# Moving one half's quantisation chain forward in a two-layer decoder kernel

## The chip, the core and the metric

The kernel runs on one core of a Trainium2 chip. The core has five engines with queues of their own: TensorE (PE, matmuls and transposes into PSUM), VectorE (DVE), ScalarE (ACT), GpSimd (POOL) and SyncE (SP), which here only issues DMAs. The engines meet at semaphores. The metric is the device time of one execution in microseconds, the median of several; smaller is better.

## The reference, cut to what matters

Two decoder layers work on x of shape (4, 256, 256), each sub-layer behind a layer norm and added to x. Only the last three sub-layers matter here:

```python
x = x + causal_attention(layernorm(x))          # 16 heads of 16, output product w_out
# cross attention, 8 groups of 2 heads of 128, everything in emulated fp8:
ln_out = ln(layernorm(x)) * ln_w + ln_b
def linear(w, w_scale, in_scale):               # four "kinds": q, qx, k, v
    y = clip(ln_out / in_scale, -448, 448)      # per column
    return (fp8(bf16(y)) * in_scale) @ w.T * w_scale
q, qx, k, v = ...                               # q, qx, k are layer normed per head
core = softmax(q k^T) v;  xout = softmax(qx kx^T) vx      # kx, vx come from the context
x = x + fp8(clip(concat(core, xout) / smooth)) @ wproj.T * scale
x = x + mixture_of_experts(layernorm(x))
```

## The kernel before, in words

The 1024 tokens are two halves of two sequences each (half 0: sequences 0 and 1, half 1: sequences 2 and 3). Each engine's program is written out by hand, and each runs its queue strictly in order. PSUM has 8 banks; the table built by `plan_front` and `plan_slot` says who uses a bank in which order, and an engine that fills a bank waits until the one before has drained it.

**Causal steps.** Causal attention runs as 16 steps (`STEPS`, i = 0 to 15, eight for each half). In one step PE makes scores for step i+1 (L744 to L748), turns the probabilities of step i (L760) and averages step i-1 (L779); DVE takes the row maxima (L1575) and copies turned probabilities (L1586); ACT takes exponentials (L1153). Among these steps half 0 gets its output product `heads_out(0)` (L705, step 10), its two layer norms Q1 and Q2, the transposes of the normed tokens (L590, step 12), and its four kinds: ACT applies ln_w, ln_b (`take_affine`, L1175) and the column scales (`scale_kind`, L1186), DVE clamps and rounds (`clamp` L1605, L1608, `round_kind` L1613, L1614), and POOL makes the last subtraction into `xq` (`split`, L1995). Every 1024-wide DVE instruction there has bf16 operands in SBUF.

**Slots.** Then 32 items (group, sequence) run through a pipeline of slots o = 0 to 35. In slot n PE projects item n (`project_item`, L835, L850; two token tiles t), turns weights of a coming group (`next_weights`, L802, L804), turns the heads of item n-1 (`turn_item_heads`, L863), makes its scores (`score_item`, L889), averages item n-3 (`average_item`, L876) and makes the output product of item n-4 (L904). ACT squares projections for the head norms (L1215), copies heads (L1224, L1231), takes exponentials (L1258) and scales averages (L1246). POOL turns the sums of squares into 1/std (`head_scale`, L1982, L1983). DVE normalises heads (L1645), takes maxima (L1659), makes the low part of each weight (L1626, L1631), scales probabilities (L1670) and lays them out by a 32x32 transpose (L1676), one for each side of the item, and quantises the averaged heads (`quantise_item`, L1652 and L113 to L116).

**The move of the probabilities.** The laid tile has a single buffer. SP moves it to `probsT` by 16 DMAs an item (`move_item_probs`, L548), after both sides are laid. DVE's side 0 transpose of the next item waits until all 16 have landed:

```python
if side == 0 and before >= 0:
    v.wait_ge(probs_moved[before % 2], (before // 2 + 1) * (16 * MOVES))
```

Items 0 to 3 belong to half 0, so half 1 has time: its output product `heads_out(1)` runs at the end of slot 0, its norms in slots 0 and 1, its token transposes in slot 2, kinds 0 and 1 in slot 2, kinds 2 and 3 in slot 3. The first item of half 1 is item 4: in slot 4 `project_item` waits for each of the four splits (kinds in the order q, k, v, qx).

## Time and profile before

| | us |
|---|---|
| median of 3 runs | 998.78 (998.55 to 1000.34) |
| the profiled execution | 998.71 |
| its span in the trace | 996.9 |
| mean granted TensorE clock | 0.966 of full speed |

The span is the stretch from the first to the last traced instruction; 1.8 us of the execution's time lie around it. All positions below are in us from the span's start. The causal steps end near 295, slot 0 starts there, and the slots fill the stretch up to about 870. A row of the timeline gives start, duration, engine, line, operation, tiles and a count of merged instructions; in brackets stands the idle time of the engine before the row and who ended it. Where instructions of one row overlap or are merged, the duration is from the first start to the last end.

### The profile page before, as it was taken

Reading aid. Unit: us, or ns where it says so; the run is one execution under the profiler, and the core shown is the slowest. Engines: PE = TensorE matmul, PEld = TensorE weight load, DVE = VectorE, ACT = ScalarE, POOL = GpSimd, SP = SyncE. Lnnn points to the kernel's source line nnn. Section 1 sums busy time; section 2 is a strip of 40 time slices with the busy share of each in tenths; the row PEclk is TensorE's granted clock in tenths of the full one; section 3 lists DMA queues with packets and bytes.
Section 4 is the critical chain, followed back from the end, with each engine's and each line's share of the span. In section 5 each row is a group of like instructions: output and inputs, shape, how many; then the busy total and the mean of one; then the engine's idle time right before and its main releaser. Section 6 shows DMA issues by size and latency. Waiting matters only on the chain.

```text
span 996.9 us, 15862 instructions
## 1 busy us (share of the span) xinstructions
PE 911.4 (91%) x5254; PEld 681.3 (68%) x5254; DVE 713.1 (72%) x1549; ACT 563.8 (57%) x2101; POOL 150.5 (15%) x194
## 2 busy tenths in 40 slices
PE   5989999998879679999999999999999998789796
PEld 3647566656558567888888787878787776545453
DVE  3674545666686886887888788888888787765653
ACT  3461335446345856777877676877777776321311
POOL 2001202000033331121212111121212121000000
PEclk9999999999889879999999999999999999889898
DMA  7001000000101312232432432423422623110000
GB/s 218 1 23 42 0 1 1 2 1 1 43 1 43 85 43 55 73 94 71 113 94 55 112 81 59 129 54 75 117 70 54 198 57 78 47 43 0 22 0 21
DMA packets 64083, 56.80 MB, mean 57 GB/s; under 512 B 11201, under 2 KB 62978, under 8 KB 64002
## 3 DMA queue, kind: packets, MB, share of 16 engines
q1 hardware_dynamic: 63904, 55.76, 20.7%
q8 instruction: 42, 0.69, 0.3%
q14 instruction: 39, 0.32, 0.1%
q10 hardware_dynamic: 98, 0.03, 0.0%
HBM read 21.15 MB, written 1.05 MB: 22 GB/s over the span
## 4 chain that ended last, share of the span: by engine, by line
PE 43%; DVE 24%; SPq 18%; issue 5%; DMA 5%; ACT 4%; POOL 2%; DVEq 0%; ACTq 0%
SPq L548 18%; DVE laid L1676 6%; PE ps L956 6%; DMA group_probsT<-laid 4%; PE ps L876 4%; PE ps L835 3%; DVE group_probs L1670 3%; PE ps L889 3%; PE ps L692 2%; PE ps L682 2%; PE ps L904 2%; PE ps L705 2%; DVE neg_max L1575 2%; PE ps L850 2%; PE ps L744 2%
## 5 line engine op out<-in xcount | busy, mean ns | idle before, releaser
L1258 ACT ACTIVATE group_probs<-ps,score_bias 128x256 f32<-128x256 f32 x256 | 117.2, 484 | 55.9 <-DVE score_bias L1659 55.9
L835 PE MATMUL ps<-group_w_hi,xq 128*128 128x256 f32 (+1 forms) x512 | 133.4, 301 | 5.5 <-POOL xq L1995 5.5
L1659 DVE TENSOR_REDUCE score_bias<-ps 128x2 f32<-128x512 f32 x128 | 87.7, 691 | 59.8 <-PE ps L889 59.8
L876 PE MATMUL ps<-group_probsT,group_values 128*128 128x512 f32 x256 | 120.8, 608 | 5.1 <-DVE x_all L1683 3.0
L835 PE MATMUL ps<-group_w_lo,xq 128*128 128x256 f32 (+1 forms) x512 | 122.9, 282 | 0.0
L1215 ACT ACTIVATE group_squares<-ps 128x128 f32<-128x128 f32 x384 | 108.7, 340 | 16.4 <-PE ps L835 9.2
L889 PE MATMUL ps<-group_kT,group_qT 128*128 128x256 f32 x512 | 115.9, 379 | 0.0
L889 PEld LDWEIGHTS ps<-group_kT,group_qT 128*128 128x128 f32 x512 | 97.0, 190 | 26.6 <-issue 10.5
L835 PEld LDWEIGHTS ps<-group_w_hi,xq 128*128 128x128 f32 x512 | 100.1, 196 | 7.1 <-issue 5.6
L835 PEld LDWEIGHTS ps<-group_w_lo,xq 128*128 128x128 f32 x512 | 100.0, 195 | 1.0
L1215 ACT ACTIVATION_READ_ACCUMULATOR group_squares<-ps 128x1 f32 x384 | 97.5, 274 | 0.0
L1676 DVE STREAM_TRANSPOSE laid<-group_probs 128x1024 f32<-128x1024 f32 x64 | 79.7, 1246 | 17.4 <-DMA group_probsT<-laid 15.9
L876 PEld LDWEIGHTS ps<-group_probsT,group_values 128*128 128x128 f32 x256 | 45.5, 191 | 61.3 <-issue 45.1
L1246 ACT ACTIVATE group_cat_y<-ps,vec_inv 128x256 bf16<-128x256 f32 x128 | 53.5, 471 | 59.7 <-PE ps L876 59.7
L1983 POOL TENSOR_TENSOR head_rstd<-head_sum,minus_half 128x6 f32<-128x6 f32 x64 | 86.0, 1343 | 5.3
L904 PE MATMUL ps<-group_wp_hi,group_cat 128*128 128x256 f32 x256 | 70.0, 310 | 8.9 <-DVE group_cat L116 8.9
L1670 DVE TENSOR_SCALAR group_probs<-group_probs,score_inv 128x256 f32<-128x256 f32 x256 | 74.6, 355 | 0.5
L1982 POOL TENSOR_SCALAR head_sum<-head_sum 128x6 f32<-128x6 f32 x64 | 13.9, 218 | 401.9 <-ACT group_values L1217 401.8
L1645 DVE TENSOR_TENSOR group_heads<-ps,head_rstd 128x384 f32<-128x384 f32 x128 | 62.4, 544 | 14.9 <-POOL head_rstd L1983 14.9
L850 PE MATMUL ps<-group_w_x,ctxT 128*128 128x256 f32 x256 | 66.5, 382 | 0.0
L904 PE MATMUL ps<-group_wp_lo,group_cat 128*128 128x256 f32 x256 | 64.3, 288 | 0.0
L1224 ACT ACTIVATE group_qT<-ps,query_affine 128x512 f32<-128x512 f32 x64 | 50.5, 789 | 24.3 <-PE ps L863 24.3
(258 smaller groups left out, 1775.3 us busy)
## 6 DMA issues: line engine op xcount, KB each, us to landing
group_probsT<-laid SPq DMA_DIRECT2D x512, 64.0 KB, 2.1
group_raw_p<-in_L_xattn_wproj_dram SPq DMA_DIRECT2D x16, 256.0 KB, 3.4
group_raw_w<-in_L_xattn_wq_dram SPq DMA_DIRECT2D x8, 256.0 KB, 2.8
group_raw_w<-in_L_xattn_wqx_dram SPq DMA_DIRECT2D x8, 256.0 KB, 3.0
group_raw_w<-in_L_xattn_w_kv_x_dram SPq DMA_DIRECT2D x16, 128.0 KB, 3.2
x_all<-in_x_dram SPq DMA_DIRECT2D x2, 512.0 KB, 6.0
front_work<-in_ctx_dram SPq DMA_DIRECT2D x1, 1024.0 KB, 6.6
group_raw_w<-in_L_xattn_wk_dram SPq DMA_DIRECT2D x8, 128.0 KB, 3.2
```

Source lines behind the costliest of these rows:

```text
L548: sp.dma_start(c.probsT[item % 2][32 * j:32 * j + 32, :, i, :], c.probs_laid[32 * i:32 * i + 32, :, j, :]).then_inc(probs_moved[item % 2], 16)
L835: last = pe.matmul(c.ps[:, bank, at:at + width], x_, w[:, k, col:col + width], start=k == 0 and m == 0, stop=k == KD - 1 and m == 1)
L850: last = pe.matmul(c.ps[:, bank, 256:512], c.ctxT[:, b, k, t * P:(t + 1) * P], c.w_x[par][:, k, :], start=k == 0, stop=k == KD - 1)
L876: last = pe.matmul(c.ps[:, bank, :].rearrange("p (i n) -> p i n", i=BLOCKS), c.values[:, item % 4, kt, side, :], c.probsT[item % 2][:, kt, ...
L889: last = pe.matmul(c.ps[:, bank, t * S:(t + 1) * S], c.qT[:, side, h, t * P:(t + 1) * P], c.kT[:, side, :], start=True, stop=True)
L904: last = pe.matmul(c.ps[:, bank, t * D:(t + 1) * D], c.cat[:, i, t * P:(t + 1) * P], w[:, i, :], start=i == 0 and m == 0, stop=i == 3 and ...
L1215: act.activation(c.squares[:, t, 3 * i + h, :], c.ps[:, bank, h * HD:(h + 1) * HD], ACT.Square, accum_out=c.head_sum[:, t, 3 * i + h:3 * i ...
L1258: last = act.activation(c.probs[:, side, h, t, :], c.ps[:, fills.bank(name), t * S:(t + 1) * S], ACT.Exp, bias=c.score_bias[:, i:i + 1], a ...
L1659: v.tensor_reduce(c.score_bias[:, i:i + 2], c.ps[:, bank, :].rearrange("p (t n) -> p t n", n=S), AX.X, ALU.max, negate=True).then_inc(nega ...
L1670: order.mark(v.tensor_scalar(p, p, c.score_inv[:, 4 * side + i:4 * side + i + 1], None, ALU.mult))
L1676: v.transpose(laid, c.probs[:, side].rearrange("p h t (k b) -> p (h t) k b", b=32)).then_inc(probs_laid, 1)
L1983: pool.tensor_tensor(c.head_rstd[:, t, :], c.head_sum[:, t, :], c.minus_half[:, 0:6], ALU.pow).then_inc(rstd_ready, 1)
```

## The change

In the causal steps, PE's `heads_out(0)` goes behind the averages of step 10. DVE's reciprocal of step 11 (`invert_heads(9)`) goes to step 12, in front of its user. ACT's `take_affine(0)` goes from the end of step 12 to between the two pairs of exponentials of step 13, and the first scaling and clamping of half 0 behind the exponentials and maxima of step 13.

In the slots, half 1's chain starts earlier: `heads_out(1)` goes between the first and the second token tile of item 0, `add` and the Q1 moments between DVE's two tiles, the norms Q1 and Q2 to the start of slot 1, the token transposes from slot 2 to slot 1, kinds 0 and 1 to slot 1, kinds 2 and 3 to slot 2. DVE takes the weights' low parts of slots 1 to 3 in front of the laying of the probabilities. On POOL the splits stand between the head norms. Bank numbers of three weights and the step of the bank table follow.

```diff
@@ plan_slot
-    for i, (g, w) in enumerate(o.weights):
-        f.plan(W_BANKS[i], ("W", g, w))
+    for (g, w), bank in zip(o.weights, (6, 7, 6) if o.n == 0 else W_BANKS):
+        f.plan(bank, ("W", g, w))
...
-    if o.n == 2:
+    if o.n == 1:
         f.plan(4, ("xT", "Q", 1, 0))
         f.plan(7, ("xT", "Q", 1, 1))
@@ PE, visit(o)
-                    if o.weights:
+                    if o.n == 0:
+                        next_weights(o, slice(0, 2))
+                        heads_out(1)
+                    elif o.weights:
                         next_weights(o)
...
                         project_item(o, 1)
+                    if o.n == 0:
+                        next_weights(o, slice(2, 3))
                     if o.outputs:
                         output_item(o)
-                    if o.n == 0:
-                        heads_out(1)
...
-                    if o.n == 2:
+                    if o.n == 1:
                         turn_tokens("Q", 1, twice[1], normed_count("Q2"))
@@ PE, step loop
-                    if i == OUT_STEP:
-                        heads_out(0)
...
                         average(i - 1)
+                    if i == OUT_STEP:
+                        heads_out(0)
@@ ACT, visit(o)
-                    if o.n == 2:
+                    if o.n == 1:
                         take_affine(1)
                         scale_kind(1, 0)
                         scale_kind(1, 1)
-                    if o.n == 3:
+                    if o.n == 2:
                         scale_kind(1, 2)
                         scale_kind(1, 3)
@@ ACT, step loop
                         exps(i, 0)
+                        if i == QUANT_STEP + 1:
+                            take_affine(0)
                         exps(i, 1)
                         take_probs(i)
+                    if i == QUANT_STEP + 1:
+                        scale_kind(0, 0)
...
-                    if i == QUANT_STEP:
-                        take_affine(0)
-                    if i + 1 in QUANTISED:
+                    if i + 1 in QUANTISED and i > QUANT_STEP:
                         scale_kind(0, QUANTISED[i + 1])
@@ DVE, visit(o)
+                    if o.n == 0:
+                        next_weights(o, slice(0, 2))
+                        normalise_item(o, (0,))
+                        add("Yc", 1)
+                        take_moments("Q1", 1, x[1])
+                        normalise_item(o, (1,))
+                        next_weights(o, slice(2, 3))
+                        return
+                    if o.n == 1:
+                        normalise("Q1", 1, x[1], xn[1], None)
+                        take_moments("Q2", 1, xn[1])
                     if o.turns:
                         invert_sums(o, 0)
                     if o.outputs:
                         quantise_item(o)
+                    if o.n < 4:
+                        next_weights(o)
+                    if o.n == 1:
+                        normalise("Q2", 1, xn[1], twice[1], normed[1])
                     if o.turns:
                         lay_item_probs(o, 0)
                         invert_sums(o, 1)
-                    if o.weights:
+                    if o.weights and o.n >= 4:
                         next_weights(o)
...
-                    if o.n in (2, 3):
-                        clamp(1, 2 * o.n - 4)
-                        round_kind(1, 2 * o.n - 4)
+                    if o.n == 2:
+                        clamp(1, 2)
+                        round_kind(1, 2)
                     if o.scores:
                         item_max(o, 0)
                         item_max(o, 1)
                     if o.n == 1:
-                        normalise("Q2", 1, xn[1], twice[1], normed[1])
-                    if o.n in (2, 3):
-                        clamp(1, 2 * o.n - 3)
-                        round_kind(1, 2 * o.n - 3)
+                        clamp(1, 0)
+                        round_kind(1, 0)
+                        clamp(1, 1)
+                        round_kind(1, 1)
+                    if o.n == 2:
+                        clamp(1, 3)
+                        round_kind(1, 3)
@@ POOL
+                head_scale(SLOTS[1], 1)
+                split(1, 0)
+                head_scale(SLOTS[2], 0)
+                split(1, 1)
+                head_scale(SLOTS[2], 1)
+                split(1, 2)
+                head_scale(SLOTS[3], 0)
+                split(1, 3)
+                head_scale(SLOTS[3], 1)
```

Where this puts the instructions is seen best in each engine's own order. DVE from the heads of slot 1 to the laying of side 1 in slot 2 (score_bias is the maxima, front_work<-second the norm Q2, group_wp_lo the low parts of the output weights), before:

```order
L1645 TENSOR_TENSOR group_heads<-ps,head_rstd 128x384 x4
L1659 TENSOR_REDUCE score_bias<-ps 128x2 x4
L1418 TENSOR_SCALAR front_work<-second,half_mv,half_rstd 128x256 x4
L1664 RECIPROCAL score_inv<-score_sum 128x4
L1670 TENSOR_SCALAR group_probs<-group_probs,score_inv 128x256 x4
L1676 STREAM_TRANSPOSE laid<-group_probs 128x4x8x32
L1664 RECIPROCAL score_inv<-score_sum 128x4
L1631 SCALAR_TENSOR_TENSOR group_wp_lo<-ps,out_scale,group_wp_hi 128x512 x2
L1670 TENSOR_SCALAR group_probs<-group_probs,score_inv 128x256 x4
```

The same place after the change, from the maxima of slot 1 on (front_quant is the kinds of half 1; line numbers are those of the changed kernel):

```order
L1665 TENSOR_REDUCE score_bias<-ps 128x2 x4
L1611 TENSOR_SCALAR front_quant<-front_quant 128x1024
L1614 TENSOR_SCALAR front_quant<-front_quant 128x1024
L1619 TENSOR_SCALAR front_quant<-front_quant 128x1024
L1620 TENSOR_TENSOR front_quant<-front_quant 128x1024
L1611 TENSOR_SCALAR front_quant<-front_quant 128x1024
L1614 TENSOR_SCALAR front_quant<-front_quant 128x1024
L1619 TENSOR_SCALAR front_quant<-front_quant 128x1024
L1620 TENSOR_TENSOR front_quant<-front_quant 128x1024
L1670 RECIPROCAL score_inv<-score_sum 128x4
L1637 SCALAR_TENSOR_TENSOR group_wp_lo<-ps,out_scale,group_wp_hi 128x512 x2
L1676 TENSOR_SCALAR group_probs<-group_probs,score_inv 128x256 x4
```

The rounding of kinds 0 and 1 now stands between the maxima of slot 1 and the weights of slot 2; the weights have passed the laying of side 0, and the norm Q2 has gone to the start of slot 1.

POOL from the last head norm of slot 2 to that of slot 3 before (head_sum and head_rstd are one `head_scale`, xq is `split`):

```order
L1982 TENSOR_SCALAR head_sum<-head_sum 128x6
L1983 TENSOR_TENSOR head_rstd<-head_sum,minus_half 128x6
L1995 TENSOR_TENSOR xq<-front_quant 128x2x512 x2
L1982 TENSOR_SCALAR head_sum<-head_sum 128x6
L1983 TENSOR_TENSOR head_rstd<-head_sum,minus_half 128x6
```

After, the stretch from the last head norm of slot 1 to the split of kind 1:

```order
L2004 TENSOR_SCALAR head_sum<-head_sum 128x6
L2005 TENSOR_TENSOR head_rstd<-head_sum,minus_half 128x6
L2012 TENSOR_TENSOR xq<-front_quant 128x2x512
L2004 TENSOR_SCALAR head_sum<-head_sum 128x6
L2005 TENSOR_TENSOR head_rstd<-head_sum,minus_half 128x6
L2012 TENSOR_TENSOR xq<-front_quant 128x2x512
```

The four splits are now each followed by one head norm, and all four stand in front of the last head norm of slot 3.

## Rows read from the trace of the kernel before

**Rows 1.** Part 1 of the page: busy us, share of the span and instructions.

```profile
PE 911.4 (91%) x5254; PEld 681.3 (68%) x5254; DVE 713.1 (72%) x1549; ACT 563.8 (57%) x2101; POOL 150.5 (15%) x194
```

**Rows 2.** Chain of waits, 498 to 515: start, us, what (the other issues left out).

```profile
498.07 0.60 SPq L548
...
507.67 2.07 DMA group_probsT<-laid
...
509.83 1.25 DVE laid L1676
...
511.14 1.30 DVE group_wp_lo L1631 x2
512.44 1.06 DVE group_probs L1670 x4
...
513.52 1.26 DVE laid L1676
```

**Rows 3.** Timeline of SP: runs of the 16 moves of an item (L548).

```profile
352.89 69.76 SPq L548 DMA_DIRECT2D group_probsT<-laid  x64
...
480.68 11.15 SPq L548 DMA_DIRECT2D group_probsT<-laid  x16
...
651.51 45.81 SPq L548 DMA_DIRECT2D group_probsT<-laid  x48
```

**Rows 4.** Timeline of DVE: side 1 of slots 2 to 5, and of slot 10.

```profile
330.69 1.25 DVE L1676 STREAM_TRANSPOSE laid<-group_probs 128x1024 f32<-128x1024 f32 x1
...
351.62 1.25 DVE L1676 STREAM_TRANSPOSE laid<-group_probs 128x1024 f32<-128x1024 f32 x1
...
374.15 1.25 DVE L1676 STREAM_TRANSPOSE laid<-group_probs 128x1024 f32<-128x1024 f32 x1
...
393.37 1.25 DVE L1676 STREAM_TRANSPOSE laid<-group_probs 128x1024 f32<-128x1024 f32 x1
...
479.33 1.25 DVE L1676 STREAM_TRANSPOSE laid<-group_probs 128x1024 f32<-128x1024 f32 x1
```

**Rows 5.** Timeline of PE, slots 2 to 5: waits, and equal work at two clocks.

```profile
329.01 1.77 PE L863 MATMUL ps<-ident,group_heads 128*128 128x128 f32 x8 [2.13 <-DVE group_wp_lo L1631]
...
349.94 1.97 PE L863 MATMUL ps<-ident,group_heads 128*128 128x128 f32 x8 [4.70 <-DVE group_wp_lo L1631]
...
367.96 0.55 PE L835 MATMUL ps<-group_w_hi,xq 128*128 128x256 f32 x1 [3.98 <-POOL xq L1995]
...
368.95 1.91 PE L850 MATMUL ps<-group_w_x,ctxT 128*128 128x256 f32 x4
...
381.73 3.62 PE L889 MATMUL ps<-group_kT,group_qT 128*128 128x256 f32 x16
...
387.02 1.02 PE L850 MATMUL ps<-group_w_x,ctxT 128*128 128x256 f32 x4
```

**Rows 6.** Windows: busy time by engine, then granted clock, DMA share, GB/s.

```profile
352.00:372.00 20.00, 15.71 (x71) 12.66 (x71) 15.34 (x28) 12.51 (x54) 5.94 (x4) 0.84 0.22 54
```

**Rows 7.** Timelines of PE and ACT in causal steps 12 and 13.

```profile
261.43 1.08 PE L760 MATMUL ps<-ident,front_work 128*128 128x128 f32 x4 [1.84 <-DVE front_work L1586]
...
268.30 1.45 ACT L1175 ACTIVATE front_xT<-ps,vec 128x512 f32<-128x512 f32 x2 [5.10 <-PE ps L590]
...
276.07 2.58 ACT L1153 ACTIVATE front_work<-ps,neg_max 128x128 f32<-128x128 f32 x8
```

**Rows 8.** Timeline of POOL: one of the eight splits.

```profile
344.85 2.12 POOL L1995 TENSOR_TENSOR xq<-front_quant 128x1024 fp32r<-128x1024 bf16 x1 [2.27 <-DVE front_quant L1614]
```

**Rows 9.** Timeline of DVE: low parts, then instructions beside a split.

```profile
280.45 1.97 DVE L1605 TENSOR_SCALAR front_work<-front_work 128x1024 bf16<-128x1024 bf16 x1
...
328.24 1.38 DVE L1631 SCALAR_TENSOR_TENSOR group_wp_lo<-ps,out_scale,group_wp_hi 128x512 fp32r<-128x512 f32 x2
...
338.31 0.43 DVE L1605 TENSOR_SCALAR front_quant<-front_quant 128x1024 bf16<-128x1024 bf16 x1
...
344.89 3.01 DVE L1670 TENSOR_SCALAR group_probs<-group_probs,score_inv 128x256 f32<-128x256 f32 x4
```

More of the change, by code:

```diff
@@ L810, in first_weights, with next_weights @@
                     turn_weight(("W", 0, w), w)
-                def next_weights(o):
-                    for g, w in o.weights:
+                def next_weights(o, which=slice(None)):
+                    for g, w in o.weights[which]:
                         if w == 6:
@@ L1205, in take_weight, with next_weights @@
                                        ACT.Copy, scale=c.out_scale[:]).then_inc(hi_ready, 1)
-                def next_weights(o):
-                    for g, w in o.weights:
+                def next_weights(o, which=slice(None)):
+                    for g, w in o.weights[which]:
                         take_weight(("W", g, w), w, g % 2)
@@ L1633, in take_weight, with next_weights, normalise_item @@
                     fills.drain(last, name)
-                def next_weights(o):
-                    for g, w in o.weights:
+                def next_weights(o, which=slice(None)):
+                    for g, w in o.weights[which]:
                         take_weight(("W", g, w), w, g)
-                def normalise_item(o):
-                    for t in range(2):
+                def normalise_item(o, tiles=(0, 1)):
+                    for t in tiles:
                         v.wait_ge(rstd_ready, 2 * o.n + t + 1)
@@ L1685, in visit @@
                 def visit(o):
+                    if o.n == 0:
+                        next_weights(o, slice(0, 2))
+                        normalise_item(o, (0,))
+                        add("Yc", 1)
+                        take_moments("Q1", 1, x[1])
+                        normalise_item(o, (1,))
+                        next_weights(o, slice(2, 3))
+                        return
+                    if o.n == 1:
+                        normalise("Q1", 1, x[1], xn[1], None)
+                        take_moments("Q2", 1, xn[1])
                     if o.turns:
@@ L1698, in visit @@
                         add_item(o)
-                    if o.n == 1:
-                        normalise("Q1", 1, x[1], xn[1], None)
-                        take_moments("Q2", 1, xn[1])
                     if o.projects:
                         normalise_item(o)
-                    if o.n == 0:
-                        add("Yc", 1)
-                        take_moments("Q1", 1, x[1])
-                    if o.n in (2, 3):
-                        clamp(1, 2 * o.n - 4)
-                        round_kind(1, 2 * o.n - 4)
+                    if o.n == 2:
+                        clamp(1, 2)
+                        round_kind(1, 2)
                     if o.scores:
@@ L1845, in _ @@
                         take_probs(i - 1, 2)
-                    if i in QUANTISED:
+                    if i in QUANTISED and i > QUANT_STEP + 1:
                         clamp(0, QUANTISED[i])
@@ L1854, in _ @@
                     if i >= 3:
-                        if i % 2 and i < STEPS - 1:
+                        if i % 2 and i < STEPS - 1 and i != OUT_STEP + 1:
                             invert_heads(i - 2)
                         elif i % 2 == 0 and i < STEPS:
+                            if i == OUT_STEP + 2:
+                                invert_heads(i - 3)
                             take_heads(i - 3)
@@ L1868, in _ @@
                         normalise("Q2", 0, xn[0], twice[0], normed[0])
+                    if i == QUANT_STEP + 1:
+                        clamp(0, QUANTISED[i])
                     if i in QUANTISED:
@@ L1984, in head_scale @@
                                        ALU.pow).then_inc(rstd_ready, 1)
-                def visit(o):
-                    if o.projects:
-                        head_scale(o, 0)
-                        head_scale(o, 1)
                 def split(h, n):
@@ L2018, in _ @@
                     split(0, n)
-                visit(SLOTS[0])
+                head_scale(SLOTS[0], 0)
                 root_of("Q1", 1)
+                head_scale(SLOTS[0], 1)
                 root_of("Q2", 1)
-                visit(SLOTS[1])
-                for o in SLOTS[2:4]:
-                    visit(o)
-                    split(1, 2 * o.n - 4)
-                    split(1, 2 * o.n - 3)
+                head_scale(SLOTS[1], 0)
+                head_scale(SLOTS[1], 1)
[7 more added lines that the diff above has]
+                head_scale(SLOTS[3], 1)
                 for o in SLOTS[4:ITEMS]:
-                    visit(o)
+                    head_scale(o, 0)
+                    head_scale(o, 1)
                 root_of("M", 0)
```

1 line of the change is left out of this document (removed).

## Prediction

> **What bounds the kernel now.** The page says that PE is busy for 91% of the span [rows 1], so one would look for PE's waits. The chain of waits says otherwise for most of the slots. From about 480 on it runs in a loop that has hardly any PE in it [rows 2]: SP issues the 16 moves of an item (498.07 to 507.67, 9.60 us), the last one lands 2.07 us later, DVE may then lay side 0 of the next item (1.25), makes low parts of weights (1.30 here), scales side 1 (1.06), lays it (1.25), and SP starts again at 514.84. With the gaps that is 16.77 us for a round, or 15.47 without weights. As measured over ten rounds, weights and slow issues included, a round takes (651.51 - 480.68) / 10 = 17.08 us [rows 3].
>
> So look at the ends of the layings of side 1, which start the moves [rows 4]: slot 2 ends at 331.94, slot 3 at 352.87, slot 4 at 375.40, slot 5 at 394.62, slot 10 at 480.58. From slot 5 to slot 10 five rounds took 85.96 us, 17.2 each, which is the loop's own rate. From slot 3 to slot 5 two rounds took 41.75 us, and neither had weights in the loop. There the loop was not what bound: PE was late. PE's waits show why [rows 5]: 4.70 us in slot 3 before 349.94 for the low parts of weights on DVE, 3.98 us in slot 4 before 367.96 for the last split on POOL. After each the clock is low: over 352 to 372 the granted clock is 0.84 of full speed [rows 6], and the same four context matmuls take 1.91 us at 368.95 and 1.02 at 387.02 [rows 5], the first at the 1.2 GHz level, the second at 2.4.
>
> **Part 1, the causal steps.** Today ACT idles 5.10 us before `take_affine(0)` at 268.30, with the exponentials of step 13 queued behind it, and those of step 14 start at 276.07 [rows 7]. In the new order the first pair of step 13 runs in that idle time. On DVE the 1.7 us reciprocal no longer stands before the norm Q1, and PE's 1.84 us wait at 261.43 for a DVE copy [rows 7] goes. The averages of step 10 (1.4 us) fill PE time before the output product. I follow it through: the copy of step 11's probabilities 1.8 us earlier, the transposes of the normed tokens 1.7 earlier, ACT's exponentials of step 14 2.5 earlier, DVE's next copies 3.5 earlier. From there the pattern of today repeats (a clamp of step 14 stands beside a split again), so slot 0 starts 3.5 us early. It can't be less than nothing, and not more than about 5 to 7 (the ACT idle and the reciprocal).
>
> **Part 2, slots 0 and 1: the lead is spent.** PE's work is the same up to the end of slot 0 (3.5 early, near 304.4). But DVE must now do: heads t=0, add, moments, heads t=1 (waiting for POOL, whose root of Q1 goes first), a low part, norm Q1 (1.4), moments (1.8), and only then the low part of weight 3 of group 1, which ends near 312.0. PE's turned heads of slot 1 need its bank, so they end near 312.9. PE stood at 313.8 there today. The token transposes (0.9, today in slot 2) go in before the scores, which end near 320.1, as today. The lead on PE is 0 by then; DVE's maxima of slot 1 are 2.4 early.
>
> **Part 3, slot 2.** DVE now rounds kinds 0 and 1, four instructions each of 0.4 to 0.7 us, 2 us a kind, before the low parts of slot 2. The first split runs beside the second clamp. What that costs a row shows: at 344.89 four scalings take 3.01 us [rows 9] beside the split of 344.85 to 346.97 [rows 8], where they take 1.06 in the loop [rows 2]: they stand still for about 1.9 us. The clamp at 280.45 takes 1.97 us in the same way, the undisturbed one at 338.31 0.43 [rows 9]. I put 1.6 us here. The low parts then run near 328.0 to 329.3; today they start at 328.24 [rows 9]. So PE's wait in slot 2 (2.13 us before 329.01 today [rows 5], in front of the second bank of heads) stays, in size about 4 as PE gets there earlier. The laying of slot 2 comes behind the low parts, and its side 0 scalings beside split 1 (3.0 for 1.1), so it ends near 336.0, 4 us later than today. That is covered: item 0 lands at 336.1 + 9.6 + 2.1 = 347.8, and PE wants it near 351.
>
> **Part 4, slot 3.** Kinds 2 and 3 are rounded around the maxima of slot 2 (2 us a kind). The maxima are over at 342.2, where they ended at 342.7 today, exponentials end at 344.6 (today 345.2). The low parts come at once, 345.3 to 346.6, not behind a laying. PE's heads go on at 346.05 where they stood at 349.94 [rows 5]: 3.9 us won, and scores of item 3 end near 357.8 (361.8 today). On DVE the laying of slot 3: scalings to 347.7, wait to 347.8 for item 0, side 0 to 349.1, side 1's scalings beside the last split (3.0), side 1 to 353.3. **Slot 3's laying ends 0.4 us later than today's 352.87**, for all the earlier work. Its bounds: the two standstills may be absent (2 to 4 us earlier), or the lead of part 1 (3.5 later).
>
> **Part 5, slots 4 and 5: the gain.** All four splits are done by 351.4, so slot 4's products don't wait (3.98 and a small wait go), the half-clock stretch behind them goes (3.5 us more), and PE ends the scores of item 4 near 373.5; today they end at 381.73 + 3.62 = 385.35 [rows 5]. From there to the laying of slot 5 today 9.27 us pass [rows 4, 5], which would put it at 382.8. But the loop can't follow: 353.3 + 2 x 15.47 = 384.2 at best, and 2 x 17.08 = 34.2 gives 387.5 at worst (a mean round with weights). I take 16.0 a round, nearer to the round without weights that the chain shows, plus half a microsecond of slow issues: 385.3. Against 394.62 that is **9.3 us early**. The bounds are 7.1 and 10.4 for the rate alone.
>
> **Part 6, what follows.** From slot 5 on the loop runs at its 17.1 to 17.2 a round, which is what slots 5 to 10 and 10 to 20 took. PE then is 1.5 to 2.5 us ahead of the loop, and nothing is given back. So the sum is 998.7 (profiled execution; the median of the runs is 998.78) - 9.3 = **989.4 us**.
>
> **Rivals.**
> (A) The forecast, loop-bound from slot 3, 987.5 to 991.2: 0.56.
> (B) Slots 1 to 3 cost more than I count: PE's three waits there (for weight 3's bank, for the low parts in slots 2 and 3) bring the low clock with them for longer, and the kinds come later. If the laying of slot 3 slips by 2 to 6 us, the gain is 3.5 to 7.5: 991.2 to 995.2. For it: [rows 5] has the low clock after each such wait. Chance 0.20.
> (C) The standstills beside the splits are smaller. The row shows only cases where POOL started first (344.85 against 344.89). After the change DVE issues its next clamp right behind the rounding that releases the split, so DVE may be first and POOL would stand still, for 0.4 us only. Then DVE saves 2 to 4 us before slot 3's laying, and with PE following the time is 985.5 to 987.5. Chance 0.12. The Trainium skill, SBUF — State Buffer, section Who interferes with whom, says this of the shared port pair: who issues first holds it for the whole instruction and the other fully blocks. The trace agrees with its one side, at 344.89.
> (D) Nothing moves (0.2%, 2 us, is about what a measurement of this kernel can tell from no change): the first rounds of the loop lose as much as PE wins. It needs a slot 3 laying at about 361. Chance 0.05.
> (E) Slower, by one mechanism: the single laid buffer. Slot 3's side 0 waits for item 0's moves, which start only when slot 2's laying ends. That is 4 us later than today by my count. If slot 2's laying ends after 347 (11 us more than I count, 15 more than today), item 0 lands after 359, slot 3's laying ends after 362.7, and the loop starts later than it would have to for a tie; each us beyond is a us lost, 1001 to 1004. Against it: nothing in the slot takes 11 us. Chance 0.07.
>
> **How the numbers follow.** The likeliest case gives 989.4. The range 985.5 to 995 holds A, C and most of B, 0.85 of the chance. Faster by over 0.2%: A, B and C, 0.88. Within: 0.05. Slower: 0.07.
>
> **What would show it.** In the changed kernel's trace: slot 0's first product near 291.5 (part 1); the scores of item 1 ending near 320 (part 2); a DVE or POOL instruction of kinds 0 to 3 stretched to 2 us or more (C if not); side 1 layings ending near 336 (slot 2), 353 (slot 3), 369 (slot 4), 385 (slot 5); no PE wait for xq in slot 4; SP hardly waiting between moves from slot 3 on. It would be wrong if PE still waits long in slots 4 and 5, or if the layings of slots 5 to 10 take clearly more than 86 us, which would mean that the loop has a price that PE's lateness had hidden.

## The result, and the profile after

| | kernel before | kernel after |
|---|---|---|
| median of 16 runs each, us | 1000.75 (995.48 to 1004.68) | 996.77 (995.14 to 1001.17) |
| ratio to before | 1 | 0.9961, 95% interval 0.9944 to 0.9978 |
| profiled execution, us | 998.71 | 999.46 |
| its span, granted clock | 996.9, 0.966 | 997.7, 0.961 |

The change makes the kernel 3.9 us faster (2.2 to 5.6), where 9.3 us were predicted. The time predicted, 989.4 us, is 7.4 us too low, and 996.77 lies outside the range of 985.5 to 995. That the profiled execution of after is not faster than that of before is no contradiction. In it the stages up to 250 us, which the change doesn't touch, came out 3.2 us later. This row, the last add to x_all of those stages, stands in the trace of before at 249.62:

```profile
252.80 0.75 DVE L1446 TENSOR_TENSOR x_all<-x_all,ps 128x256 f32<-128x256 f32 x2 [0.98 <-PE ps L705]
```

This late start is taken for chance: a second trace of the kernel after has the row at 249.94. So from here on positions are also given as +us behind the start of this row, which takes the untouched stages out. The side 1 layings of slots 2 to 5 and of slot 10, the rows that answer to [rows 4], in the trace of after:

```profile
342.84 1.25 DVE L1682 STREAM_TRANSPOSE laid<-group_probs 128x1024 f32<-128x1024 f32 x1
...
361.43 1.25 DVE L1682 STREAM_TRANSPOSE laid<-group_probs 128x1024 f32<-128x1024 f32 x1
...
377.61 1.25 DVE L1682 STREAM_TRANSPOSE laid<-group_probs 128x1024 f32<-128x1024 f32 x1
...
393.63 1.25 DVE L1682 STREAM_TRANSPOSE laid<-group_probs 128x1024 f32<-128x1024 f32 x1
...
479.51 1.25 DVE L1682 STREAM_TRANSPOSE laid<-group_probs 128x1024 f32<-128x1024 f32 x1
```

Their ends, start plus 1.25, are 344.09, 362.68, 378.86, 394.88 and 480.76:

| end of laying, + us | predicted | before | after |
|---|---|---|---|
| slot 2 | 86.4 | 82.32 | 91.29 |
| slot 3 | 103.7 | 103.25 | 109.88 |
| slot 5 | 135.7 | 145.00 | 142.08 |
| slot 10 | 221.7 | 230.96 | 227.96 |

From slot 3 to slot 5 the two rounds took 32.20 us, where 32.0 were predicted and 41.75 stood before, and from 5 to 10 it is 85.9 as predicted. So the loop did what the prediction said. But it started 6.2 us later than predicted. Two places made that lateness.

**Step 12.** Slot 0's first product (the first L835, which the expectations below call the first product of the laid Q), which the lead of part 1 should have brought from +45.9 to +42.4, stands at +45.6. PE's rows of step 12:

```profile
269.34 1.09 PE L590 MATMUL ps<-ident,front_work 128*128 128x128 f32 x8 [3.16 <-DVE front_work L1424]
...
272.83 1.65 PE L744 MATMUL ps<-front_work 32*128 32x128 f32 x8
...
275.81 1.65 PE L744 MATMUL ps<-front_work 32*128 32x128 f32 x8
...
281.71 0.92 PE L744 MATMUL ps<-front_work 32*128 32x128 f32 x8
```

PE stood for 3.16 us for DVE's norm (L1424), a wait that part 1 had not counted. Behind it the same eight products L744 take 1.65 us at 272.83 and 275.81 and 0.92 at 281.71: the first two at the 1.2 GHz level, the last at 2.4. The trace of before has 0.92 for them at 272.56.

**Slots 1 to 3.** PE's waits and what ran behind them, the rows that answer to [rows 5]:

```profile
318.81 1.97 PE L863 MATMUL ps<-ident,group_heads 128*128 128x128 f32 x8 [1.46 <-DVE group_w_lo L1632]
...
336.75 1.97 PE L863 MATMUL ps<-ident,group_heads 128*128 128x128 f32 x8 [4.09 <-DVE group_wp_lo L1637]
...
351.32 0.63 PE L804 MATMUL ps<-ident,group_raw_p 128*128 128x128 f32 x4 [2.08 <-ACT group_probs L1261]
...
355.32 1.97 PE L863 MATMUL ps<-ident,group_heads 128*128 128x128 f32 x8 [1.10 <-DVE group_wp_lo L1637]
...
359.95 1.02 PE L850 MATMUL ps<-group_w_x,ctxT 128*128 128x256 f32 x4
```

The second and third of the three heads banks (L863 x8) take 1.97 us behind each of the waits in slots 1, 2 and 3; undisturbed, all three (x12) take 1.47 at 375.02. Four context matmuls take 1.02 at 359.95, at the 2.4 GHz level again. Windows of the same stretches (busy time by engine, then granted clock, DMA share, GB/s), the first before slot 3, the second as in [rows 6], the last from slot 4 on:

```profile
330.00:345.00 15.00, 10.91 (x57) 9.97 (x56) 14.68 (x25) 11.10 (x49) 6.50 (x6) 0.77 0.12 37
352.00:372.00 20.00, 18.61 (x94) 15.31 (x95) 17.07 (x31) 16.06 (x75) 5.13 (x5) 0.83 0.32 86
372.00:395.00 23.00, 21.88 (x131) 17.76 (x130) 18.36 (x39) 16.24 (x75) 6.17 (x8) 1.00 0.23 58
```

The clock is 0.77 over 330 to 345 and 0.83 over 352 to 372. The same work stands about 3 us earlier in the trace of before; there it is 0.89 over 326.8 to 341.8 and 0.84 over 348.8 to 368.8. So the low clock behind the waits of slot 4 went, and new low clock came in slots 1 and 2. As a sum nothing was won. The first 96 us from slot 0's first product on, in before and in after:

```profile
295.52:391.52 96.00, 79.34 (x464) 68.34 (x461) 71.95 (x150) 62.65 (x279) 29.80 (x31) 0.91 0.21 56
298.37:394.37 96.00, 82.86 (x486) 71.74 (x483) 76.69 (x156) 64.99 (x284) 31.41 (x33) 0.91 0.21 56
```

The granted clock is 0.91 in both. The wait for splits in slot 4 (3.98 us in [rows 5]) has gone, as predicted.

### The profile page after: what moved, and what is told of

Read it like the earlier page. It is cut to its first block, busy times and chain, and to the rows that moved or that the text cites. A ratio compares the mean times of both kernels' runs of the same rounds, so it can differ in the third digit from the quotient of the medians.

```text
span 997.7 us, 15862 instructions
## 1 busy us (share of the span) xinstructions
PE 915.0 (92%) x5254; PEld 685.9 (69%) x5254; DVE 715.3 (72%) x1549; ACT 564.3 (57%) x2101; POOL 150.1 (15%) x194
## 4 chain that ended last, share of the span: by engine, by line
PE 40%; DVE 25%; SPq 21%; DMA 5%; issue 5%; ACT 3%; POOL 1%; DVEq 0%
SPq L548 21%; DVE laid L1682 6%; PE ps L959 5%; DMA group_probsT<-laid 5%; DVE group_probs L1676 3%; PE ps L876 3%; PE ps L835 2%; PE ps L692 2%; PE ps L682 2%; PE ps L889 2%; PE ps L705 2%; PE ps L904 2%; PE ps L670 2%; DVE neg_max L1581 2%; PE ps L744 2%
## 5 line engine op out<-in xcount | busy, mean ns | idle before, releaser
L835 PE MATMUL ps<-group_w_hi,xq 128*128 128x256 f32 (+1 forms) x512 | 132.8, 300 | 1.2 <-POOL xq L2012 1.2
L835 PE MATMUL ps<-group_w_lo,xq 128*128 128x256 f32 (+1 forms) x512 | 122.6, 282 | 0.0
L1218 ACT ACTIVATE group_squares<-ps 128x128 f32<-128x128 f32 x384 | 108.6, 339 | 16.1 <-PE ps L835 12.5
L835 PEld LDWEIGHTS ps<-group_w_hi,xq 128*128 128x128 f32 x512 | 99.9, 195 | 2.4 <-issue 1.5
L835 PEld LDWEIGHTS ps<-group_w_lo,xq 128*128 128x128 f32 x512 | 99.8, 195 | 0.9
```

What stands on the lines that cost most here:

```text
L835: last = pe.matmul(c.ps[:, bank, at:at + width], x_, w[:, k, col:col + width], start=k == 0 and m == 0, stop=k == KD - 1 and m == 1)
L1218: act.activation(c.squares[:, t, 3 * i + h, :], c.ps[:, bank, h * HD:(h + 1) * HD], ACT.Square, accum_out=c.head_sum[:, t, 3 * i + h:3 * i ...
```

## Experiments

The theory after the first look (T): the loop passes on what the laying of slot 3 wins, and 6 us were lost ahead of it to PE's low clock behind waits, about 3 in step 12 and 3 in slots 1 to 3. Its rivals: the loss is in POOL and DVE standing beside each other; the loop or the tail gives the gain back.

### The two parts apart

e1_steps is the kernel before with the order of steps 10 to 13 of the change alone, e2_slots the kernel before with the slots' part alone.

> Before plus the causal-step part of the change alone (order of steps 10 to 13), slots as in before. The prediction held this part for 3.5 us of lead at slot 0; the profile after shows 0.35 us. In the kernel before the next standing waits of slots 0 to 3 stand behind it. Theory T (the lead was lost inside step 12 to PE running at the 1.2 GHz level after a 3.2 us wait): this kernel is 0 to 0.6 us faster than before, ratio 0.9994 to 1.0000, and its first product of the laid Q of kind 1 comes less than 1 us earlier, measured from the end of the x_all adds near 250 us. If the prediction's Part 1 was right after all and the slots lost it: that product is 3 us or more earlier and the kernel up to 3 us faster.

> Before plus the slots part of the change alone (new order of slots 0 to 4 on PE, DVE, ACT and GpSimd), causal steps as in before. Theory T: the step part brought 0.35 us, so this kernel has nearly the whole gain: 3 to 4.5 us faster than before (ratio 0.9955 to 0.9970). If the slot part needs the lead of the step part, as the prediction's sum had it: its gain is that of after less 3.5 us, about 0 to 0.5 us.

Measured: e1_steps 0.9972 (0.9956 to 0.9988), 2.8 us faster, and not 0 to 0.6. e2_slots 0.9966 (0.9947 to 0.9985), 3.4 us faster, as expected. The two add up to 6.2, which is above the first interval of what after brought (2.2 to 5.6) and inside that of its second comparison below (3.6 to 7.7). In the trace of e1_steps the first product of slot 0 stands at +45.92, no earlier than in before's trace, just as T said, and yet the kernel gained. So something was wrong with before's trace as the yardstick. That was looked at next.

### The kernels before and after once more

> The kernel before, unchanged: what the measurement makes of no change at all, and a second trace of it. Theory and rival agree on a ratio of 1.000 whose interval takes in 1. The trace tells whether the unchanged stages up to 250 us come out at one time or at two (the x_all adds of the last of these stages stood at 247.9 us in before and 251.1 us in after).

> The kernel before, unchanged, a third trace. In the first the products of step 12 behind PE's wait for the exponentials ran at the 2.4 GHz level from 272.6 us and the first product of the laid Q of kind 1 came 45.9 us after the last x_all add, in the second they ran at 1.2 GHz until 280 us and it came 49.1 us after. Theory C (chance of the clock decides 3.2 us here in before, and the prediction was made on a run where it fell well): again one of these two, 45.9 or 49.1, within 0.3 us. Rival: a continuum in between.

> The kernel after, unchanged, beside the others on the same chip. Theory T: about 0.996 of before, and by its second trace the same low-clock stretches behind PE's wait in step 12 and in slots 1 to 3 (they come from the order of the work, not from the run). Rival (they were chance of one run): the second trace shows them at the 2.4 GHz level and the laying of slot 5 comes 3 us or more earlier, measured from the x_all adds near 250 us.

Measured: before_again 1.0003 (0.9985 to 1.0021); after_again 0.9944 (0.9923 to 0.9964), that is 5.6 us. The eight products L744 of step 12 in the first and in the second trace of the kernel before, which has the same wait of 2.04 us ahead of them:

```profile
272.56 0.92 PE L744 MATMUL ps<-front_work 32*128 32x128 f32 x8 [2.04 <-ACT front_work L1153]
```

```profile
272.34 1.65 PE L744 MATMUL ps<-front_work 32*128 32x128 f32 x8 [2.04 <-ACT front_work L1153]
...
282.05 0.92 PE L744 MATMUL ps<-front_work 32*128 32x128 f32 x8
```

In the first trace they run at 2.4 GHz at once, in the second at 1.2 GHz until about 282 us. In both the granted clock had been low once already, until about 268. In the first it then falls again at about 275, for 3 us; in the second it falls at about 272, for 10 us. The first product of slot 0 in three traces of before, two of after:

| + us | before | before_again | before_third | after | after_again |
|---|---|---|---|---|---|
| first L835, slot 0 | 45.90 | 49.12 | 49.00 | 45.57 | 45.93 |
| laying of slot 3 | 103.25 | 106.67 | 106.53 | 109.88 | 110.79 |
| laying of slot 5 | 145.00 | 148.96 | 147.44 | 142.08 | 142.95 |
| end of the span | 747.28 | 751.18 | 751.60 | 744.90 | 744.56 |

Theory C held, as far as three traces tell: two values and nothing between. e2_slots above and e17_before_order below have the same steps 10 to 13, and fit: their first product stands at +46.13 and +49.05. The execution that the prediction read was one in which the clock had come back 3.2 us sooner than in the other two. The prediction's base of 998.7 was low by 2.0 us against the median of before in the comparison with the change (1000.75), and by 3.0 to 4.2 against those of the later comparisons (1001.7 to 1002.9). Set against the two slower traces, the change wins 3.1 to 3.6 us at slot 0, so part 1 does bring what it said, measured from them. Slots 0 to 3 then lose 7 instead of the predicted 4, and at slot 5 4.5 to 6.9 us are won. The second trace of after has its low clock in the same places as the first (L744 1.65 us at 270.44 and 273.41). e1_steps has it there too (L744 1.65 us at 270.52 and 273.50). So in after's order of the steps it came in every trace looked at, while in before's the second low comes short or long by chance.

### PE kept busy in its waits

e3_fill_step is after with work for PE that nobody reads, in front of the norm's wait; e4_fill_all has more of it in slots 1 to 3.

```diff
+                def keep_busy(name, count):
+                    bank = fills.claim(pe, name)
+                    for _ in range(count):
+                        pe.transpose(c.ps[:, bank, 0:P], c.ident[:], c.ident[:])
...
+                        keep_busy(("xT", "Q", 0, 0), 22)
```

> After plus 22 transposes of the identity on PE (results never read) in step 12, ahead of the transposes that wait for the Q norm. They stand in PE's wait of 3.2 us, so PE does not stand idle there. Theory T: the products behind the wait then run at the 2.4 GHz level (L744 0.9 us for 8 and not 1.65), the first product of the laid Q of kind 1 comes 2 to 3 us earlier than in after, and the kernel is 2 to 3 us faster than after if slots 1 to 3 pass it on (0.25% on top of after's 0.39%: ratio to before 0.993 to 0.995). Rival (the lead is lost to DVE and ACT, not to the clock): the same as after or slower by what the transposes push back, 0 to 1 us. Second rival: the lead is won at slot 0 and lost again at the low clock of slots 1 to 3: product earlier, time as after.

> As e3_fill_step, plus transposes of the identity in PE's waits of slots 1, 2 and 3 (10, 30 and 8 before the second pair of head products, and 15 before the weight products of slot 3). Theory T: low clock in these slots costs 3 us, so the layings of slots 2 and 3 come about 3 us earlier than in e3, and the kernel is 2 to 3 us faster than e3: ratio to before 0.990 to 0.992, that is the predicted 9.3 us. Rival (in these slots the chain through DVE, ACT and GpSimd sets the layings): no change against e3. Rival (the fills are longer than the waits): up to 2 us slower than e3.

Measured: e3_fill_step 0.9931 (0.9907 to 0.9955), 1.3 to 3.0 us less than after by the two ratios of after (0.9944 and 0.9961). The intervals overlap, so the time alone doesn't show this gain; the trace does, at slot 0. PE in its step 12 (L749 is after's L744):

```profile
262.97 2.62 PE L596 MATMUL ps<-ident 128*128 128x128 f32 x22
...
266.20 1.09 PE L590 MATMUL ps<-ident,front_work 128*128 128x128 f32 x8 [0.61 <-DVE front_work L1430]
...
270.67 0.92 PE L749 MATMUL ps<-front_work 32*128 32x128 f32 x8
```

The 22 transposes take 2.62 us, the wait that is left is 0.61, and the eight products take 0.92. Slot 0's first product comes at +42.74, and part 1 had it at +42.4. The granted clock is 0.94 over 262 to 280, where after has 0.72 over 265 to 283. e4_fill_all, e4_again and e15_fill_order have the same 22 transposes and their first product at +42.59, +42.85 and +42.55. So the step 12 half of T is shown: the missing lead at slot 0 was the low clock. Not all of it lasts. The laying of slot 2 comes 1.3 us earlier than in after (2.0 than in after_again), that of slot 3 2.2 us (3.1).

e4_fill_all came out at 0.9934 (0.9910 to 0.9959), no faster than e3, where 2 to 3 us were expected. Its laying of slot 3 did come 2.8 us earlier, at +104.81 for e3's +107.65, which is 1.1 us behind the predicted 103.7. So the slots' half of T is right up to slot 3. But the laying of slot 5 stands at +138.79 for e3's +140.27, and that of slot 10 at +227.36 for +226.29. The gain was lost between, and a second look was taken at it.

> The kernel with transposes in PE's waits of step 12 and of slots 1 to 3 again, for a second trace: its laying of slot 3 came 2.8 us earlier than in the kernel that fills step 12 alone, and at slot 10 nothing of that was left. If the moves of laid probabilities hold the rounds from slot 3 on (theory L): layings of slots 3 to 6 again 16.8 us or more apart, DVE waiting for a DMA at the first laying of slot 4 for over 3 us, ratio 0.993. If it was chance of one run (slow DMAs): rounds of 16.1 us as elsewhere, ratio 0.990 to 0.991.

Measured: 0.9920 (0.9894 to 0.9945), 992.1 us, between the two ratios expected. Layings of slot 3 at +105.12, of slot 4 at +122.33, of slot 5 at +139.35: rounds of 17.2 and 17.0, though neither has weights in the loop. The first laying of slot 4 in this trace, with its wait for the moves:

```profile
368.40 1.25 DVE L1692 STREAM_TRANSPOSE laid<-group_probs 128x1024 f32<-128x1024 f32 x1 [3.94 <-DMA group_probsT<-laid]
```

The chain of waits between the layings of slots 3 and 4 has SP's issues, the landing and DVE's work around the layings, and no PE: in after 16 issues of about 0.60 us, the longest 0.74, in e4_again one of 1.73 and another with 0.44 us beside it. What slowed these issues I did not find; e4_fill_all has one of 1.54 in the same round, and e15_fill_order, below, one of 1.67. PE's two waits in slot 4 show what the round means for it, first for the landing, then for the add that stands behind the layings on DVE:

```profile
368.39 1.96 PE L883 MATMUL ps<-group_probsT,group_values 128*128 128x512 f32 x4 [1.45 <-DMA group_probsT<-laid]
...
372.79 2.74 PE L883 MATMUL ps<-group_probsT,group_values 128*128 128x512 f32 x4 [2.44 <-DVE x_all L1699]
```

So with PE early, the moves hold this round and PE stands for 3.9 us. From 372.79 to the laying of slot 5 the chain goes through PE's products: the 17.0 of the second round is PE's, late by its wait. A little of the clock goes again too:

```profile
360.00:380.00 20.00, 16.11 (x80) 12.03 (x79) 12.57 (x26) 10.65 (x49) 3.07 (x4) 0.91 0.29 71
```

### The second scaling taken out of the loop

The round from move to move had, beside 16 issues and the landing, laying of side 0, reciprocal, scaling of side 1 and laying of side 1. The scalings need no move. So DVE can make both ahead of its wait:

```diff
                     if o.turns:
+                        scale_item_probs(o, 0)
+                        invert_sums(o, 1)
+                        scale_item_probs(o, 1)
                         lay_item_probs(o, 0)
-                        invert_sums(o, 1)
                     if o.weights and o.n >= 4:
                         next_weights(o)
                     if o.turns:
                         lay_item_probs(o, 1)
```

(Shortened: this order in slots from 3 on; the scaling no longer stands in the laying.)

> As e4_fill_all, and in the slots from 3 on DVE scales both sides of the probabilities before it waits for the moves, so that between the end of an item's moves and the start of the next ones only the two layings stand (2.5 us and not 3.8). Theory L (the moves hold the rounds after the slots' waits are filled): rounds of slots 3 to 6 up to 1.2 us shorter, 1 to 3 us faster than e4_again. Rival P (from slot 4 on PE is the bound, 19.9 of 20 us busy, and all that could be won before is won): same as e4_again within 0.2%.

> The kernel after, with the scaling of both sides before the wait for the moves (and the layings one behind the other), without any fill. If the fills and the scaling order act apart: 996.5 less what the order gives, 987 to 991 us (0.986 to 0.991 of before). If the order helps only where the fills have already brought the layings forward: 995 to 997 us, as after.

Both leave out the scaling of the last item, 2.3 us in the tail, so their times are up to that much too short. Measured: e8_scale_first 982.9 us, 0.9808 (0.9792 to 0.9825), 9.2 us below e4_again. Less the 2.3 us that is 6.9, where theory L had 1 to 3 and rival P nothing: P is out, and L too small. e11_after_scale, without fills, came to 991.8 us, 0.9887 (0.9858 to 0.9915): the order helps without fills too. Four more leave out the same scalings. With fills, a wait (e10_scale_wait), a reciprocal (e12_recip_between) or one of the scalings (e13_scale_between) stood between the two layings: 0.9803, 0.9852 and 0.9863. e14_after_scale, as e13_scale_between without fills, came to 0.9889. Their intervals are 0.3 to 0.4% to either side, so what stands there is worth 0.6% at most, and more the runs don't tell. The last three kernels are whole:

> After, with the fills of e4_fill_all, and in every slot from 3 on DVE scales both sides before it waits for the moves; the last item's scalings, which e8_scale_first and e11_after_scale left out (2.3 us in the tail), stand in it. Theory L (from slot 3 on the moves hold the rounds where PE has time to spare): e8_scale_first's time and at most those 2.3 us: 983 to 986 us, 0.981 to 0.985 of before. Rival P (PE is the bound from slot 4 on): 991 to 993 us as e4_again.

> The kernel after with the same order of scalings and no fills. Theory L: e11_after_scale's 991.8 us and at most 2.3 us of the last item's scalings, 989 to 993 us, 0.987 to 0.992 of before, so 4 to 7 us less than after alone. Rival: as after, 996 to 997 us.

> The kernel before with the same order of scalings in every slot from 3 on. Theory L: rounds of slots 4 to 7 up to 1.2 us shorter as in e11_after_scale, later rounds where a DMA is waited for too: 995 to 999 us, 0.993 to 0.998 of before, and the change of this case then still brings 4 to 6 us on top (e16_after_order). Rival: before has no wait for the moves worth the name, 1001 to 1003 us.

| | without the order | with the order |
|---|---|---|
| before | 1 | 0.9963 (0.9938 to 0.9987) |
| after | 0.9961 and 0.9944 | 0.9895 (0.9873 to 0.9916) |
| after with fills | 0.9934 and 0.9920 | 0.9845 (0.9821 to 0.9868) |

All three ratios fell where theory L put them, and all three times lie outside those of the rivals. In microseconds e16_after_order (992.9) did too; e15_fill_order (987.9) came 1.9 us above its 983 to 986 and e17_before_order (999.2) 0.2 above its 995 to 999. The layings in e15_fill_order (two in one row, 2.37 us), of slots 4 and 5, and the window in which PE stood for 3.9 us in e4_again:

```profile
368.37 2.37 DVE L1694 STREAM_TRANSPOSE laid<-group_probs 128x1024 f32<-128x1024 f32 x2 [1.00 <-DMA group_probsT<-laid]
...
383.57 2.37 DVE L1694 STREAM_TRANSPOSE laid<-group_probs 128x1024 f32<-128x1024 f32 x2
```

```profile
360.00:380.00 20.00, 19.86 (x122) 16.58 (x121) 16.39 (x34) 15.38 (x73) 3.19 (x4) 1.00 0.32 79
```

Rounds from slot 3 on are 15.7 and 15.2 us; slot 5 is laid at +133.39, 6.0 us before e4_again; PE is busy for 19.86 of 20 us at full clock. Which of the two, moves or PE, holds the kernel after slot 5? In the table of groups the waits of all 64 layings are, in e4_again and in e15_fill_order (busy, mean ns, idle before):

```profile
L1692 DVE STREAM_TRANSPOSE laid<-group_probs 128x1024 f32<-128x1024 f32 x64 | 79.7, 1246 | 21.6 <-DMA group_probsT<-laid 20.1
```

```profile
L1694 DVE STREAM_TRANSPOSE laid<-group_probs 128x1024 f32<-128x1024 f32 x64 | 78.1, 1235 | 2.1 <-DMA group_probsT<-laid 1.0
```

And the chain that ended last, by engine, from the pages of after and e16_after_order (without fills), then of e4_again and e15_fill_order (with fills):

```profile
PE 40%; DVE 25%; SPq 21%; DMA 5%; issue 5%; ACT 3%; POOL 1%; DVEq 0%
```

```profile
PE 67%; DVE 22%; ACT 5%; issue 4%; POOL 1%; DMA 0%; DVEq 0%
```

```profile
PE 50%; DVE 23%; SPq 15%; issue 4%; DMA 3%; ACT 3%; POOL 1%; DVEq 0%
```

```profile
PE 64%; DVE 24%; ACT 5%; issue 4%; POOL 1%; SPq 1%; DMA 1%; DVEq 0%
```

With the scalings out of the loop the moves leave the chain, from 21% to nothing and from 15% to 1%, and PE takes their place. But the 28 rounds from slot 5 to slot 33 take 475.5 us in e15_fill_order and in e16_after_order, and 478.0 in e4_again, 479.7 in after and 476.9 in after_again: 0.05 to 0.15 us a round, for 1.3 us less in the loop. So the loop through the moves was the longer one there, but by a tenth of a microsecond; the loop through PE is right behind it. Where PE has caught up and can run ahead, in slots 3 to 5 with fills, the new order wins more: the laying of slot 5 comes 6.0 us before e4_again's. Without fills e16_after_order wins 1.0 to 1.9 us up to slot 5, has hardly any of it at slot 10 (+227.96, for after's +227.96 and after_again's +228.38), and wins 3.3 to 5.2 up to slot 33.

e15_fill_order, at 987.9 us (986.14 to 988.7), is 1.55% faster than before and, by the ratios, 1.0 to 1.2% faster than after. It beats both.

## Why the prediction was wrong

The step that failed is the clock behind PE's waits. Part 1 gave a lead of 3.5 us and 0.33 came, and parts 2 to 4 let the work behind PE's waits in slots 1 to 3 run as if a wait cost only its own length. Together the laying of slot 3, from which part 5 counts, came 6.2 us later than predicted.

**What bounds the kernel** was half right. The loop of [rows 2] is there, and from slot 3 to slot 5 it does hold the rounds once PE is in time. For the rounds from slot 5 on the prediction took the moves for the bound because the chain between 498 and 515 goes through them. The chain from 380 to 480 of that same trace, which it didn't read, has products on top and no move among its larger parts. From 480 to 650 the moves do lead it. So the 85.96 us of slots 5 to 10, which the prediction calls the loop's own rate, were PE's. The two stretches (by line, shares of the stretch):

```profile
by line: PE ps L876 20.5%; PE ps L889 19.0%; PE ps L835 18.4%; PE ps L904 9.5%; PE ps L850 8.6%; PE ps L863 6.5%; PE ps L802 4.9%; DVE laid L1676 2.5%; DVE group_probs L1670 2.1%; ACT group_probs L1258 1.6%; DVE group_wp_lo L1631 1.3%; DVE 
```

```profile
by line: SPq L548 55.4%; DVE laid L1676 14.7%; DMA group_probsT<-laid 12.7%; DVE group_probs L1670 6.3%; issue 4.8%; DVE group_w_lo L1626 3.6%; DVE group_wp_lo L1631 2.3%; DVE score_inv L1664 0.4%; SPq L545 0.1%; DVEq L1674 0.1%
```

**Part 1** foresaw 3.5 us, and the trace showed 0.33. This is the term that failed first. PE's new wait for the norm (3.16 us) was not in the working: the prediction removed PE's 1.84 us wait for a copy, and did not ask what PE would wait for next. With the low clock behind it this cost 2.8 to 3.2 us at slot 0, and e3_fill_step got them back there. The prediction also took its base from one execution, in which PE's second low in this stretch happened to be short; in two others of the same kernel it isn't, and against those the change does win 3.1 to 3.6 us here.

**Part 2** (lead 0 at the scores of slot 1, near 320.1) and **Part 3** (slot 2 laid near 336): the scores of item 1 ended at +75.65 for +70.5, and slot 2 was laid at +91.29 for +86.4. The fills show what these 5 us are. At the scores step 12's fill gives back 1.3 (e3_fill_step, +74.31) and slot 1's 2.7 more (e4_again, +71.58). At slot 2's laying it is 1.3 (+89.95) and 2.7 to 3.0 (+87.27 and +86.98). So more than half was low clock behind PE's waits in slot 1 (1.46 us before 318.81), which the sum had at nothing. The standstills beside splits were taken rightly: 1.6 for a clamp, 1.9 for four scalings. The rows of after, DVE, POOL, DVE:

```profile
332.10 0.42 DVE L1611 TENSOR_SCALAR front_quant<-front_quant 128x1024 bf16<-128x1024 bf16 x1
332.27 2.23 POOL L2012 TENSOR_TENSOR xq<-front_quant 128x1024 fp32r<-128x1024 bf16 x1 [5.51 <-DVE front_quant L1620]
332.56 2.22 DVE L1614 TENSOR_SCALAR front_quant<-front_quant 128x1024 uint16<-128x1024 uint16 x1
337.27 3.03 DVE L1676 TENSOR_SCALAR group_probs<-group_probs,score_inv 128x256 f32<-128x256 f32 x4
```

The clamp at 332.10 was first and took its 0.42; the split of 332.27 then went on, and the next DVE instruction took 2.22, where the same one took 0.43 at 330.57. The scalings took 3.03 for the 1.06 of [rows 2]. So **rival C** did not come, and being first saved DVE a single instruction here. The Trainium skill, SBUF — State Buffer, section Who interferes with whom, says of the shared port pair that who issues first holds it for the whole instruction and the other fully blocks. These rows agree, 2.22 us to a split of 2.23.

**Part 4**, slot 3 laid 0.4 us later than before: it was 6.6 later, 6.2 more than predicted. Step 12's fill gave back 2.2 of these (3.1 against after_again), and the fills of slots 1 to 3 another 2.8 and 2.5 (e4_fill_all and e4_again). The 1.1 to 1.4 us that are left were not looked for. PE stood for 4.09 us before 336.75 (about 4 was predicted for slot 2) but the prediction let the products behind run at full speed. It knew the price, since it counted 3.5 us for the half-clock stretch of slot 4 as won. It did not charge with it the waits of slots 1 to 3, which the new order left standing or made longer. The windows above give the same clock over the first 96 us of the slots, 0.91 in before and after: the 3.5 us were not won as a sum, they moved.

**Part 5** was right where it was tested: 16.1 us a round for 16.0, no wait for splits in slot 4. Only its start was late. e4_fill_all and e4_again, which start 1.1 and 1.4 us behind the predicted 103.7, show that the predicted start would not have brought the predicted end: their rounds were 17.0 to 17.2. The bounds of 7.1 and 10.4 us there give 988.3 to 991.6, and not the 987.5 to 991.2 that A has.

**Part 6** was right in number (85.9 us from slot 5 to slot 10), but for slots 5 to 10 wrong in cause, as said above.

**Rival B**, with a chance of 0.20, is nearest to what happened: PE's waits in slots 1 to 3 bring the low clock, and its gain of 3.5 to 7.5 us holds the 3.9 and 5.6 measured. It had the laying of slot 3 slip by 2 to 6 us; it slipped by 6.2, since B lacked step 12. Its time of 991.2 to 995.2 missed since it was counted from an execution 2 to 4 us under the usual. D and E did not come.

## What to carry to other kernels

A wait that is removed from a busy matrix engine is replaced by the next one; write down what that is, and charge every wait that stays with the clock behind it. One profiled execution is one throw: where a stretch of it runs at full clock behind a wait, a second trace shows whether that is the rule, and the sum should be made against the usual one. Before a loop is called the bound, read the chain of waits in several stretches. Where two loops run at nearly one speed, taking 1.3 us out of one shortens a round by about 0.1 us only, and over 28 rounds that is still 3 us. On top of after, by the means of the ratios, fills for PE alone brought 2.6 us, the scalings out of the moves' loop alone 5.8, and both together 10.8; that the two bring more together than apart (8.4) is within the intervals.

## What was not expected of the hardware

- The clock in the same stretch of the same kernel: with 2.04 us of wait ahead of L744, PE ran at 2.4 GHz in one execution of before, and in two others at 1.2 GHz for about 10 us. Slot 0 started at +45.9 or at +49.0 to +49.1 and nothing between.
- Transposes of a 128x128 identity that nobody reads, 22 in 2.62 us, kept the 2.4 GHz level through a wait of 3.2 us and brought slot 0 2.8 to 3.2 us forward.
- The stages ahead, up to the last add to x_all, bring that row at about 249.4 to 250.1 us or at about 252.5 to 253.1 us, in executions of one and the same kernel too (249.94 and 252.80 for after). Why is open.
- Two layings one behind the other take 2.37 us, and not 2.50.
- Issues of 0.60 us on SP's queue have a slow one of up to 1.73 us among them, in three traces with fills in the same round (1.54, 1.73 and 1.67); this was seen and not explained.
